# Idle products at the start of a fused transformer kernel, a first embedding by parts, and a new order of its first loads

## The reference

```python
h = L0_tok(x)                    # 16 images 3x128x128, patches of 16: 64 tokens of width 192
    # embed patches, layernorm, + positions -> x0
    # ff (192 -> 768 -> 192, gelu tanh), attention of 12 heads, + x0 -> x2
    # ff again (the same weights), + x2
h = concatenate([h, txt], 1)     # 64 + 32 = 96 tokens
h = h + L0_attn(layernorm(h))    # short convolution with gates, attention, ff
h = h + L0_ffn(layernorm(h))     # attention of 12 heads of 64 with gates of experts
```

## Time and profile before

| | us |
|---|---|
| median of three runs | 570.95 |
| lowest and highest run | 568.47, 573.49 |
| span of the profiled execution | 569.6 |
| TensorE busy in it | 515.9 (91%) |
| VectorE busy | 406.6 (71%) |
| ScalarE busy | 299.0 (52%) |
| GpSimd busy | 97.0 (17%) |

### The profile page before, as it was taken

The page is one execution under the profiler, slowest core; times in us unless marked ns, Lnnn a source line. Parts: engine busy times, 40 slices in busy tenths (PEclk is TensorE's granted clock), DMA queues, the critical chain, the costliest instruction groups (busy, mean ns, idle before and its releaser), DMA issues.

```text
span 569.6 us, 11352 instructions
## 1 busy us (share of the span) xinstructions
PE 515.9 (91%) x4673; PEld 396.6 (70%) x4673; DVE 406.6 (71%) x891; ACT 299.0 (52%) x488; POOL 97.0 (17%) x85
## 2 busy tenths in 40 slices
...
PEclk9799999979999999999999999999998999999999
...
DMA packets 12675, 16.02 MB, mean 28 GB/s; under 512 B 6235, under 2 KB 10048, under 8 KB 12240
## 3 DMA queue, kind: packets, MB, share of 16 engines
...
q10 hardware_dynamic: 2400, 2.00, 1.1%
q0 software_dynamic: 512, 0.59, 0.6%
...
## 4 chain that ended last, share of the span: by engine, by line
PE 70%; DVE 17%; ACT 7%; issue 3%; POOL 1%; DMA 1%; ACTq 0%; DVEq 0%; POOLq 0%
PE ps L692 16%; PE ps L1005 9%; PE ps L702 8%; PE ps L682 7%; PE ps L825 4%; PE ps L783 3%; DVE smax L1715 3%; DVE pr L1741 3%; PE ps L1066 2%; PE ps L1180 2%; DVE psum L1729 2%; PE ps L1202 2%; PE ps L1156 2%; PE ps L1056 2%; PE ps L840 2%
## 5 line engine op out<-in xcount | busy, mean ns | idle before, releaser
L1715 DVE TENSOR_REDUCE smax<-ps 96x12 f32<-96x1152 f32 (+1 forms) x28 | 37.8, 1351 | 18.1 <-PE ps L1056 10.8
L1729 DVE TENSOR_REDUCE psum<-pr 128x12 f32<-128x1152 f32 (+1 forms) x24 | 32.3, 1344 | 4.3 <-ACT pr L1371 4.3
L1366 ACT ACTIVATE pr<-ps,less 128x96 f32<-128x96 f32 (+1 forms) x96 | 24.6, 337 | 17.9 <-DVE less L1717 17.8
L1409 ACT ACTIVATE squares<-ps 128x1536 f32<-128x1536 f32 x12 | 17.4, 1450 | 27.5 <-PE ps L702 21.6
L1957 POOL TENSOR_TENSOR side_wide<-attn,w_mask 128x1024 f32<-128x1024 f32 (+1 forms) x12 | 20.7, 1748 | 59.1 <-ACT attn L1261 47.4
L1828 DVE TENSOR_REDUCE ss<-squares 128x24 f32<-128x1536 f32 x12 | 21.0, 1749 | 12.1 <-ACT squares L1409 12.1
L1983 POOL TENSOR_TENSOR squares<-squares,qk_root 128x512 f32<-128x512 f32 x8 | 16.7, 2082 | 75.0 <-DVE qk_root L1504 75.0
L1931 POOL TENSOR_TENSOR ln_root<-ln_root,minus_half 128x3 f32<-128x3 f32 x8 | 6.8, 856 | 129.5 <-DVE ln_root L1603 129.5
L682 PE MATMUL ps<-w_cqkv,side_c 64*96 64x384 f32 (+1 forms) x96 | 27.4, 500 | 0.0
L1005 PE MATMUL ps<-w_ff,b_kB 128*128 128x192 f32 x144 | 25.5, 329 | 0.0
L692 PE MATMUL ps<-w_cqkv,side_c 128*128 128x512 f32 (+1 forms) x72 | 25.0, 492 | 0.0
...
## 6 DMA issues: line engine op xcount, KB each, us to landing
x_in<-in_xT SPq DMA_DIRECT2D x3, 768.0 KB, 4.5
...
```

Source lines behind the costliest of these rows:

```text
L1366: m = act.activation(e[:, s % 2, h * N:(h + 1) * N], t[0:rows, h // 4, h % 4 * N:(h % 4 + 1) * N], ACT.Exp, scale=head ** -0.5, bias=less[ ...
L1715: dve.tensor_reduce(mx, t, AX.X, ALU.max).then_inc(w.S[stage + "_sub"], 1)
L1729: dve.tensor_reduce(psum[0:rows, s % 2, :], e, AX.X, ALU.add).then_inc(w.S[done], 1)
```

## The change

It adds nine products, warm.4 to warm.12, on a tile that POOL sets to 1.0 (the first 256 columns of bT, which is written again later): four ahead of d_em, four behind it and one behind d_x0. It moves a_bc from ahead of d_x0 to behind it. The products of d_em run part by part over both tiles instead of tile by tile. w_patch_b gets a semaphore of its own, and the addition of tok_b to w_pe moves from ahead of d_en into d_x0 on DVE. tff1 is issued right behind w_patch_b, the six tables behind tproj, and POOL issues tqkv behind the power of d_en instead of at its start. The rest of STEPS_TEXT keeps its order; only its line breaks change.

```diff
-    d_en:0 d_em:0=7 a_bc=7 d_x0:0=7 d_f1.0:0=1 a_en:1 a_em:1=4 d_f2.0:0=5 d_h2.0:0=2 a_x0:1=4 d_qk:0=5 a_f1.0:1=2
+    warm.4=0 warm.5=1 warm.6=2 warm.7=3 d_en:0 d_em:0=7 warm.8=0 warm.9=1 warm.10=2 warm.11=3 d_x0:0=6 warm.12=5
+    a_bc=4 d_f1.0:0=1 a_en:1 a_em:1=4 d_f2.0:0=5 d_h2.0:0=2 a_x0:1=4 d_qk:0=5 a_f1.0:1=2 d_v:0=6 d_e.0:0 d_s.0:0
...
@@ -374,6 +374,7 @@
         b_vB_all = heads[:, 4 * TB:].rearrange("p (s h d) -> p s h d", s=GS, h=NH)
         c_v_all = heads[:, 0:2 * NH * HD2].rearrange("p (b h d) -> p b h d", b=2, h=NH)
         b_vB, c_v = b_vB_all[0:N], c_v_all[0:N]
+        idle = bT[:, 0, 0:256]
         b_kB = sb("b_kB", [128, 2 * 2 * 6 * N])
         b_kBv = b_kB[:, 0:2 * 2 * TB].rearrange("p (o c t) -> p o c t", o=2, c=2)
         w_parity = sb("w_parity", [128, 2])
@@ -445,9 +446,9 @@
                 seconds = [second for second, first in SHARED.items() if first == name]
                 S[name] = sem("_then_".join([name] + seconds))
         S.update({name: S[first] for name, first in SHARED.items()})
-        loads = {n: sem("load_" + n) for n in ("patch0", "patch1", "patch2", "vec", "tables", "tff1", "tff2", "tqkv", "tproj", "in", "out", "qkv",
+        loads = {n: sem("load_" + n) for n in ("patch0", "patch1", "patch2", "patch_b", "vec", "tables", "tff1", "tff2", "tqkv", "tproj", "in", "out", "qkv",
                                                "proj", "ff1", "ff2", "cqkv", "cproj", "ident", "cols")}
-        n_loads = {"patch0": 2, "patch1": 2, "patch2": 2, "vec": 9, "tables": 6, "tff1": 4, "tff2": 1, "tqkv": 16, "tproj": 4, "in": 4, "out": 1, "qkv": 16,
+        n_loads = {"patch0": 2, "patch1": 2, "patch2": 2, "patch_b": 1, "vec": 8, "tables": 6, "tff1": 4, "tff2": 1, "tqkv": 16, "tproj": 4, "in": 4, "out": 1, "qkv": 16,
                    "proj": 2, "ff1": 4, "ff2": 1, "cqkv": 6, "cproj": 6, "ident": 1, "cols": 12}
         s_set = sem("constants_set")
         s_mean = sem("weight_mean")
@@ -457,6 +458,7 @@
         s_ones = sem("ones_row")
         s_pad = sem("zeros")
         s_first_part = sem("first_part_of_bank")
+        s_idle = sem("idle_operand")
 
         class Where:
 
@@ -611,19 +613,19 @@
                 j = slice(2 * part, 2 * part + 2)
                 sp.dma_start(w_patch[:, j, :], patchT[:, j]).then_inc(loads[f"patch{part}"], 16)
             sp.sem_inc(S["early_x_in"], 16)
-            sp.dma_start(w_patch_b[:], patch_b).then_inc(loads["vec"], 16)
+            sp.dma_start(w_patch_b[:], patch_b).then_inc(loads["patch_b"], 16)
+            lapped_rows(sp, "tff1", w_tff1, tok_ff1)
             sp.dma_start(w_ident[:, :], ident).then_inc(loads["ident"], 16)
             lapped_rows(sp, "vec", w_pe, peT)
-            sp.wait_ge(s_pad, 2)
-            for dst, src in ((v128[:], vec128), (w_mask[0:HC, 0:6], mask), (w_mask[HC:128, 6:8], mask[0:128 - HC, 0:2]),
-                             (w_prio[:], prio), (w_ff2_b[:], ffn2_b), (w_cproj_b[:], cproj_b)):
-                sp.dma_start(dst, src).then_inc(loads["tables"], 16)
-            lapped_rows(sp, "tff1", w_tff1, tok_ff1)
             sp.dma_start(w_tff2[:], tok_ff2).then_inc(loads["tff2"], 16)
             sp.dma_start(x_in[:, :, :], xT[1]).then_inc(S["x_in"], 16)
             for rows in (slice(0, HC), slice(HC, HC + 1)):
                 sp.dma_start(w_tproj[rows, :, 0:128], tok_proj[rows, :, 0:128]).then_inc(loads["tproj"], 16)
                 sp.dma_start(w_tproj[rows, :, 128:256], tok_proj[rows, :, 64:D]).then_inc(loads["tproj"], 16)
+            sp.wait_ge(s_pad, 2)
+            for dst, src in ((v128[:], vec128), (w_mask[0:HC, 0:6], mask), (w_mask[HC:128, 6:8], mask[0:128 - HC, 0:2]),
+                             (w_prio[:], prio), (w_ff2_b[:], ffn2_b), (w_cproj_b[:], cproj_b)):
+                sp.dma_start(dst, src).then_inc(loads["tables"], 16)
             text(sp, 0, S["early_txt_in"])
             lapped_rows(sp, "in", w_in, in_proj)
             sp.dma_start(w_out[:], out_proj).then_inc(loads["out"], 16)
@@ -776,12 +778,16 @@
                 for sem_read, value in reads_before(w, ("a_em", 0)):
                     pe.wait_ge(sem_read, value)
                 t = slot(w, ("a_em", 0))
-                for tile in range(TILES_A):
-                    for j in range(KP):
-                        if w.chain == "d" and tile == 0 and j % 2 == 0:
-                            pe.wait_ge(loads[f"patch{j // 2}"], 32)
-                        m = pe.matmul(t[:, tile * D:(tile + 1) * D], w.x.x_in[:, j, tile * 128:(tile + 1) * 128],
-                                      w_patch[:, j, :], start=(j == 0), stop=(j == KP - 1))
+                steps = [(tile, j) for tile in range(TILES_A) for j in range(KP)]
+                if w.chain == "d":
+                    steps = [(tile, j) for part in range(3) for tile in range(TILES_A) for j in (2 * part, 2 * part + 1)]
+                for n, (tile, j) in enumerate(steps):
+                    if w.chain == "d" and n % 4 == 0:
+                        pe.wait_ge(loads[f"patch{j // 2}"], 32)
+                    opens = j == 0 and (w.chain != "d" or tile == 0)
+                    closes = j == KP - 1 and (w.chain != "d" or tile == TILES_A - 1)
+                    m = pe.matmul(t[:, tile * D:(tile + 1) * D], w.x.x_in[:, j, tile * 128:(tile + 1) * 128],
+                                  w_patch[:, j, :], start=opens, stop=closes)
                 m.then_inc(fill_sem(w, ("a_em", 0)), 1)
 
             def a_x0(w, _):
@@ -1215,7 +1221,12 @@
                 for sem_read, value in reads_before(w, ("warm", k)):
                     pe.wait_ge(sem_read, value)
                 t = slot(w, ("warm", k))
-                if w.first:
+                if k > 3:
+                    if w.first:
+                        pe.wait_ge(s_idle, 1)
+                    pe.matmul(t[:, 0:256], idle[:, 0:128], idle, start=True, stop=True)
+                    return
+                if k == 2:
                     pe.wait_ge(loads["ident"], 16 * n_loads["ident"])
                 pe.matmul(t[:, 0:2 * D], w_ident[:, :], w_patch[:, 0:2, :], start=True, stop=True)
 
@@ -1471,10 +1482,7 @@
                 for t in (e_vB, a_vB):
                     m = dve.memset(t[64 * odd:64 * odd + 64, :, :, c:c + 1], 1.0)
             m.then_inc(s_set, 1)
-            dve.wait_ge(loads["vec"], 16 * n_loads["vec"])
-            for c in range(2):
-                dve.tensor_scalar(w_pe[:, c, :], w_pe[:, c, :], split_col("tok_b", c), None, ALU.add).then_inc(s_set, 1)
-            dve.wait_ge(s_set, 5)
+            dve.wait_ge(loads["patch_b"], 16 * n_loads["patch_b"])
 
             def powered(w, name, group, done, starts):
 
@@ -1527,6 +1535,12 @@
 
             def a_x0(w, _):
 
+                if w.chain == "d":
+                    dve.wait_ge(loads["vec"], 16 * n_loads["vec"])
+                    for c in range(2):
+                        dve.tensor_scalar(w_pe[:, c, :], w_pe[:, c, :], split_col("tok_b", c), None, ALU.add)\
+                           .then_inc(s_set, 1)
+                    dve.wait_ge(s_set, 5)
                 dve.wait_ge(fill_sem(w, ("a_x0", 0)), fill_count(w, ("a_x0", 0)))
                 t = slot(w, ("a_x0", 0)).rearrange("p (c s t) -> p c s t", c=2, s=GS)
                 for c in range(2):
@@ -1918,11 +1932,11 @@
 
         @block.gpsimd
         def _(pool):
+            pool.memset(idle, 1.0).then_inc(s_idle, 1)
             pool.memset(minus_half[:, :], -0.5).then_inc(s_half, 1)
             pool.memset(bias_rows[:, :], 0.0).then_inc(s_pad, 1)
             pool.memset(w_mask[:, :], 0.0).then_inc(s_pad, 1)
             pool.memset(c_kT[0:HC, 0:2, 0:2 * (HC + 1)], 0.0).then_inc(s_pad, 1)
-            split_rows(pool, "tqkv", w_tqkv, tok_qkv, cols=HEAD_PARTS)
             pool.wait_ge(s_half, 1)
 
             def power(w, tile, n, name, group, k):
@@ -1932,6 +1946,8 @@
 
             def a_en(w, _):
                 power(w, w.x.a_root, TILES_A, "a_root", w.a, 1)
+                if w.chain == "d":
+                    split_rows(pool, "tqkv", w_tqkv, tok_qkv, cols=HEAD_PARTS)
 
             def a_ht(w, _):
                 power(w, w.x.root["x_root"], 2 * TILES_B, "x_root", w.a, 2)
```

More of the change, by code:

```diff
@@ L70 @@
 STEPS_TEXT = """
-    d_en:0 d_em:0=7 a_bc=7 d_x0:0=7 d_f1.0:0=1 a_en:1 a_em:1=4 d_f2.0:0=5 d_h2.0:0=2 a_x0:1=4 d_qk:0=5 a_f1.0:1=2
[L72 to L84, removed]
-    b_f1.1:1=0 a_ht:2 b_f2.0:1=7 c_pt.0:0 b_f2.1:1=6 c_qt.2:0=2 a_u:2 b_f2.2:1 c_o.0:0=1 c_pt.1:0=3 c_s.2:0 c_e.2:0
@@ L86 @@
-    c_s.3:0=5 c_e.3:0 c_v.2:0 c_n.2:0 a_in.0:2 a_cv.0:2 c_o.1:0=4 a_in.1:2=0 a_cv.1:2 c_v.3:0=6 c_n.3:0 c_pt.2:0=3
-    a_gt.0:2 c_pr.0:0 c_o.2:0=5 c_pt.3:0 a_gt.1:2 a_cv.2:2 c_pr.1:0=4 c_o.3:0=5 a_gt.2:2 a_out.0:2=7 a_out.1:2=1
-    a_out.2:2=4 a_em:3=3 b_u.1:2=5 a_en:3 c_pr.2:0=7 c_u:1 b_qk:2 b_v:2=6 a_x0:3 b_s.0:2=2 b_s.1:2 b_e.0:2 b_n.0:2
-    b_e.1:2 b_n.1:2 warm.3 a_f1.0:3 a_f2.0:3 a_h2.0:3=7 b_pt.0:2=1 b_s.2:2 b_e.2:2 b_n.2:2 a_qk:3=2 a_v:3=0 c_g:1=1
```

(6 more changed lines are left out.)

42 lines of the change are left out of this document (28 added, 14 removed).

## The result

| | before | after |
|---|---|---|
| median of eight runs, us | 570.28 | 567.07 |
| lowest and highest | 568.47, 573.49 | 565.36, 574.92 |
| ratio after/before, 95% interval | | 0.9931 [0.9908, 0.9955] |
| span of the profiled execution, us | 569.6 | 564.7 |

The ratio leaves disturbed executions out; 0.9931 of 570.28 is a gain of 3.9 us, 0.7%. It lies outside the 569.1 to 572.2 of my forecast and inside the range of 564.0 to 573.5 only because that range reached towards rival 2; that it held is luck more than insight.

The account below looks back on a forecast made before the run. TensorE is busy for most of the span, with transfers second; w_cproj's landing leaves 1.8 us of a 6.3 us early gain, less 1.5 for a clock fall: 570.95 - 0.3 = 570.6, own range 569.1 to 572.2, full range 564.0 to 573.5.

Parts of the forecast that it names:

- rival 2: At a_wc.0: w_cproj lands some 5 us earlier or its shown landing is too late; all 6.3 us come through, 564.6; chance 0.18.
- w_cproj keeps its place behind the same bytes: it lands at 58.2 again: At a_wc.0 on VectorE: reached at 53.0, it still waits for w_cproj until 58.2, leaving 1.8 of 6.3 us.
- the queues are full from 2 us on: Weight transfers: all 16 DMA engines busy from 2 to 46 us, share 1.06, so w_cproj cannot land earlier.
- my cap: At a_wc.0: the wait for w_cproj until 58.2 leaves 1.8 us of the 6.3 us gained earlier.
- The rule of the Trainium skill: Transfer tail after 46 us: w_cqkv's 95-row and 1-row transfers use five engines and one, so no reordering shortens it.
- clock rises: Kernel start: idle products warm.4 to warm.7 bring TensorE's full clock at 7.2 us, bounds 5.5 and never.
- embedding done: First embedding, part by part with early clock: done at 10.2 us against 13.86, giving 3.7 us (bounds 1.0 and 4.1).
- first feed-forward: First 12 feed-forward records at full clock take 2.86 instead of 5.12 us, bringing the shift to 6.6 us.
- x_in[1] lands: Group 1's x, issued at 7.3 instead of 10.35, lands near 20.0; TensorE wants it at 19.6, costing 0.3 us.
- last of tqkv lands: At d_qk: tqkv, issued by GpSimd until 21.3, lands at 27; wanted at 29.6, so hidden by 2.6 us.
- Rival 4: At d_qk: tqkv lands late, free until 34.0; at 41.8 it is 5.9 us too late, time 576.8; chance 0.07.
- The clock fall at d_f1.1: Before d_f1.1 TensorE idles 4.4 us and the clock falls, costing 0 to 3.0 us, taken as 1.5.

Follow-up runs that it names:

- tqkv first: The changed kernel with tqkv issued by GpSimd at its start, as before the change; ratio to the kernel before 0.996 [0.9933, 0.9988].
- one later profile: The changed kernel with tqkv issued from ScalarE's queue and w_cproj on a semaphore of its own; ratio to the kernel before 0.9905 [0.9868, 0.9941].

## Why the prediction was right in range and wrong in mechanism

The step that failed is "w_cproj keeps its place behind the same bytes: it lands at 58.2 again". It landed at 51.8, the whole early gain came through at a_wc.0 (59.33 - 53.01 = 6.3 us), and rival 2, to which I gave 0.18, is what happened, short of the 564.6 it named. The forecast of 570.6 gave a gain of 0.3 us where 3.9 was measured; only the width of the stated range covered that. Two readings were wrong in it.

First, "the queues are full from 2 us on" came from a DMA share of 1.06 over 2 to 46 us. A share says that engines are occupied, not what they move. From 7 to 11 us the old order moved 151 GB/s at a share of 1.27, less than half of the 337 before it. The new one moves 264 there and 320 against 224 in the five microseconds behind; less what the old order catches up until 22 us it is 0.6 MB ahead, or 2.5 us at the 244 GB/s that both kernels move from 22 to 40 us. That is about the size of the 2 us by which w_cproj comes earlier in the new order (mostly 51 to 52.3 against 53.9 in two of three old ones). SP also comes to its large loads sooner, to w_cqkv at 18.33 instead of 20.32 us; but with tqkv first it was 21.05, and w_cproj still landed at 51.8, so the earlier issue is not what brings it. Which move brings the rate is open: with one group of small pieces put back it was 244 and 218 GB/s and w_cproj landed as after, with tff1 late as well it was 160 and 53.9. The early tff1 is thus as good a candidate as the small pieces, and no run moves it alone.

Second, I took a landing from one execution as a constant. The second profile of the same kernel has it at 53.9. So of the 6.4 us between the first two profiles, 58.2 - 53.9 = 4.3 us is the kernel's own spread, and 2.1 us are left for the order. The 4.5 us that my cap took away (6.3 - 1.8) were of the size of that spread.

The rule of the Trainium skill that I had set beside it ("DMA: Bandwidth & Descriptors", section "Why a DMA increments its semaphore by 16 and not by 1": as many of the 16 engines as divide the slow dimension) is neither shown nor spoken against: a tail at a low share is there in both kernels (0.44 and 0.28), and no row shows the engines of one transfer. For the transfer of one row it does not plainly give the one engine that I took: it goes by the slowest dimension larger than one. And it says nothing on when the tail ends, and I let it stand as support for a fixed end.

Term by term:

| step | predicted | measured |
|---|---|---|
| clock rises | 7.2 us | about 4.7 (4.36 us for 24 records); about 7 in one later profile |
| embedding done | 10.2 | 9.03 |
| first feed-forward | 15.4, 2.86 us long | 14.25, 2.86 |
| wait of a_bc for bias rows | 0 to 0.4 | 0.40, under the writing of x0T |
| x_in[1] lands | 20.0 | 15.7 |
| last of tqkv lands | 27, no wait | 29.5, wait 2.27 |
| a_wc.0 reached | 53.0 | 53.01 |
| w_cproj lands | 58.2 | 51.8 |
| end of kernel, gain | 0.3 | 3.9 (spans: 4.9) |

In the profile of the kernel after the idle products did what was asked of them, at no cost and earlier than I said. The clock was the term I mis-sized by 2.5 us, because no row of before showed TensorE dense from its first microseconds; it also varies, since one later profile has it at about 7 us behind the same products. x_in[1] came 4.3 us before my time: 8.2 us from issue to landing where I worked from 12.2. tqkv came later: its last piece took 9.97 us, not the 5.7 of the earlier trace rows, issued as it now is among SP's large loads; issued by ScalarE, the last piece goes out at 17.6 us and nothing waits for it. The predicted 53.0 at a_wc.0 was thus met by two errors that cancel: the gain at group 1 was 7.7 us, not 6.3, and the tqkv wait took back 1.4. Rival 4 named this wait and its place, but with a threshold of 34.0, below which w_cproj was to cover it; with that cover gone each microsecond beyond 28.2 (29.59 - 2.27 + 0.89) costs.

The clock fall at d_f1.1 that took 1.5 us of my sum never came, for want of the idle time: d_f1.1 started at 58.13, 6.3 us earlier, with no stop ahead of it. The gain did shrink late, by about 1.3 us, at a spell near 428 us, for which I had no term.
